# Decoder layer on one core: the context's rounding and that of two batches moved beside the attention

## The chip, the cores and the metric
The kernel runs on one core of one Trainium2 chip. The metric is the time of one execution on the device in microseconds (us), lower is better. Engines are named TensorE (PE in the rows, PEld its weight loads), VectorE (DVE), ScalarE (ACT), GpSimd (POOL) and SyncE (SP, which issues nearly all transfers).

## What is computed
One decoder layer on x, four batches of 512 tokens, width 512, in float32. Cut to what matters:

```python
x = x + attention(layernorm(x), wq, wk, wv, wo)    # 32 heads, 8 key heads, head width 64, rotary, causal
xq = quant_dequant_act_1x128(layernorm(x))         # q = (xb * 448/amax).astype(float8_e4m3fn), back to float32
wq = quant_dequant_weight_128x128(ctx)             # the same, amax over blocks of 128x128 of the context
x = x + einsum('emk,enk->emn', xq, wq)             # each batch with its own context, 512x512
x = x + moe(layernorm(x), ...)                     # 8 experts, top 1, capacity 256, plus a shared feed-forward, width 704
```

The rounding to an 8-bit float is done in float32: the tile is scaled, a step is formed from each element's exponent, the step (a large number) is added and taken away again, and the tile is scaled back.

## The kernel before
All matrix products are made of three products of high and low halves, so most results go through a copy (high half, ScalarE) and a subtraction (low half, VectorE or GpSimd). Each engine has its own program, written out by hand; order within an engine is the order of the code, and engines meet at semaphores. `Once` leaves out a wait whose value was already waited for.

**Attention.** A unit is a group of four query heads of one batch. There are 32 units, so NH = 128 heads, and batches 0 and 1 are complete after unit 15. All engines run the loop `for h in range(-8, NH + 7)`. In iteration h TensorE makes the scores of head h in four blocks (lines 418, 419), a part of the projections of a unit two units ahead (400 to 402), the product with the values of head h-3 (457, 458), the turns of the probabilities of head h-2 (442) and the output of an earlier head. VectorE masks the four score blocks (994), joins halves (1029), makes the low halves of the turned probabilities (1035), adds to X (1044), and once in eight heads splits weights (973). ScalarE takes the exponentials (742) and the high halves (754), and after the probabilities the pair's high half OTh (764). GpSimd normalises the probabilities (1390), rotates queries and keys and makes low halves (1428 for OTl). Projections end with iteration 119.

**The second part.** It follows a table, `slots()`, which gives stages numbers s. Up to s = -9 they run in iteration h = s + 143 of the attention loop (h from NH-11 = 117), three after it, and from s = -5 on beside `ffn(x, k)`, with s = 8x + k - 5; x counts groups of 256 tokens of the shared feed-forward, then experts. For each batch b, 16 slots apart, the stages are:
- `context_max` (1069): the largest magnitudes of the four context tiles, then `context_all` (1454): one `partition_all_reduce` on GpSimd, then `context_scales`. The context is loaded a second time for the rounding.
- `context_round`, per tile: VectorE scales it (1056), isolates the exponent (1062) and forms the step (1064), and GpSimd adds, subtracts and scales back (1433, 1435, 1437); then `context_turn`, four transposes on TensorE (392), a copy on ScalarE (770), a subtraction on VectorE (1106).
- `stats2`, `norm2`: mean and variance of X after attention; `cross_round`, per tile: norm (943), magnitudes (1095), scales (1047 to 1052), and the same rounding; then `cross_turn` and `cross_product`.
- norms, turns and choice of the expert for the routing.

The tiles of the second part live in `work`, whose memory is shared with the attention's tiles. `T1[0]` is also the source of zeros that SyncE writes to `xd`, the experts' input in DRAM, in iterations 116 to 123 (line 1683). `xnx`, two tiles in the attention's memory, is used for the first norms of X only. The first norms and turns of batches 2 and 3 run in iterations 51 to 59.

## Time and profile before

| | us |
|---|---|
| median of 3 runs | 1612.6 (1609.4 to 1612.7) |
| the profiled execution | 1614.8 |
| its span in the profile | 1613.0 |
| TensorE busy | 1467.1 |
| VectorE busy | 1237.6 |
| GpSimd busy | 1058.6 |
| ScalarE busy | 917.9 |

The span is cut in the text by time from its start. Heads of attention run from about 55 to 1020 us, the second part begins beside the last of them at 913 us, and the experts follow at about 1360 us. Busy is time in which an engine executed something; a busy TensorE is not one at its peak, and its granted clock, given for each window as a share of 2.4 GHz, tells how fast it went.

### The profile page before, as it was taken

To read this page: it belongs to the slowest core of one execution; us is meant where nothing else is said; L and a number is where in the kernel's file an instruction comes from. 1 tells how busy PE (TensorE), PEld (TensorE's weight loads), DVE (VectorE), ACT (ScalarE), POOL (GpSimd) and SP (SyncE) were. 2 spreads that over 40 slices of the span, in tenths; PEclk is the share of its full clock that TensorE was granted. 3 is DMA by queue.
4 is the path that set the end of the run, shared out by engine and by line. 5 is a ranking of instruction groups with operands and counts; after the bars stand their busy time and mean duration, and the time that the engine had idled before them with its cause. 6 is when DMAs were issued, how large, how long until landed. Compare 5 with 4: busy or idle time off the path is not lost.

```text
span 1613.0 us, 26858 instructions
## 1 busy us (share of the span) xinstructions
PE 1467.1 (91%) x8616; PEld 1290.2 (80%) x8616; DVE 1237.6 (77%) x2986; ACT 917.9 (57%) x2277; POOL 1058.6 (66%) x1040
## 2 busy tenths in 40 slices
PE   5899999999989999999999967728889898899997
PEld 4688888888878888888888856627778787899996
DVE  6787787788887787788787879858797964677785
ACT  2587777777667777777777655422121213566562
POOL 1798888888776888888888767626252522444545
PEclk9899999999999999999999988969989899899998
DMA  5322232222312222232322333031101003577767
GB/s 189 87 73 66 81 76 71 77 81 55 81 50 63 75 74 66 81 89 55 82 76 59 112 119 92 8 125 41 52 27 53 7 27 113 160 234 221 226 209 239
DMA packets 78796, 152.13 MB, mean 94 GB/s; under 512 B 15366, under 2 KB 15622, under 8 KB 78656
## 3 DMA queue, kind: packets, MB, share of 16 engines
q1 hardware_dynamic: 76096, 142.16, 30.3%
q0 software_dynamic: 2560, 8.25, 1.5%
q8 instruction: 70, 1.15, 0.3%
q14 instruction: 70, 0.57, 0.1%
HBM read 87.58 MB, written 16.78 MB: 65 GB/s over the span
## 4 chain that ended last, share of the span: by engine, by line
PE 74%; DVE 12%; issue 6%; POOL 4%; ACT 2%; DMA 1%; SPq 1%; DVEq 0%; POOLq 0%; ACTq 0%
PE bank L400 15%; PE bank L401 15%; PE bank L402 15%; PE bank L442 7%; PE bank L418 5%; PE bank L457 5%; PE bank L458 5%; PE bank L419 4%; PE bank L392 2%; DVE work L943 1%; POOL P L1390 1%; DVE work L1056 1%; DVE aam L1095 1%; PE bank L429 1%; DVE st L938 1%
## 5 line engine op out<-in xcount | busy, mean ns | idle before, releaser
L742 ACT ACTIVATE P<-P,mn 128x512 f32<-128x512 f32 (+3 forms) x512 | 284.5, 556 | 221.6 <-DVE mn L994 220.9
L1390 POOL TENSOR_TENSOR P<-P,ri 128x128 f32<-128x128 f32 (+3 forms) x512 | 353.9, 724 | 10.4 <-DVE ri L983 10.4
L994 DVE CUSTOM_DVE_ANT_0 P<-bank,mask 128x512 f32<-128x512 f32 (+3 forms) x512 | 235.6, 479 | 118.3 <-PE bank L419 117.9
L1035 DVE TENSOR_TENSOR PTl<-bank,PTh 128x512 fp32r<-128x512 f32 (+1 forms) x384 | 229.2, 598 | 37.0 <-ACT PTh L754 33.9
L442 PE MATMUL bank<-ident,P 128*128 128x128 f32 x1280 | 203.4, 274 | 7.2 <-POOL P L1390 7.2
L754 ACT ACTIVATE PTh<-bank 128x512 fp32r<-128x512 f32 (+1 forms) x384 | 197.6, 516 | 6.0 <-PE bank L442 2.9
L418 PE MATMUL bank<-KT,QT 128*128 128x256 f32 (+2 forms) x512 | 191.2, 373 | 7.4 <-DVE mn L994 7.3
L457 PE MATMUL bank<-PTh,VS 128*128 128x256 f32 (+2 forms) x512 | 164.5, 332 | 11.5 <-DVE PTl L1035 8.8
L400 PE MATMUL bank<-XT,Wh 128*128 128x512 f32 x384 | 165.4, 431 | 9.6 <-DVE qcs L1007 4.7
L419 PE MATMUL bank<-KT,QT 128*128 128x256 f32 (+2 forms) x512 | 167.3, 327 | 0.0
L1428 POOL TENSOR_TENSOR OTl<-Opair,OTh 128x512 fp32r<-128x512 f32 x64 | 83.5, 1305 | 120.8 <-ACT OTh L764 120.5
L458 PE MATMUL bank<-PTl,VS 128*128 128x256 f32 (+2 forms) x512 | 157.4, 329 | 0.0
L442 PEld LDWEIGHTS bank<-ident,P 128*128 128x128 f32 x1280 | 150.9, 141 | 8.0 <-POOL P L1390 7.9
L401 PE MATMUL bank<-XT,Wh 128*128 128x512 f32 x384 | 153.9, 401 | 0.0
L402 PE MATMUL bank<-XT,Wl 128*128 128x512 f32 x384 | 153.8, 401 | 0.0
L1468 POOL TENSOR_TENSOR Ul<-RW,Uh 128x512 fp32r<-128x512 f32 x50 | 73.1, 1465 | 119.4 <-ACT Uh L791 112.0
L457 PEld LDWEIGHTS bank<-PTh,VS 128*128 128x128 f32 x512 | 98.4, 192 | 31.9 <-issue 14.1
L400 PE MATMUL bank<-XT,Uh 128*128 128x256 f32 x352 | 103.7, 295 | 17.2 <-ACT XT L770 10.6
L813 ACT ACTIVATE hm<-bank 128x256 f32<-128x256 f32 x96 | 36.3, 378 | 145.4 <-PE bank L402 133.7
L418 PEld LDWEIGHTS bank<-KT,QT 128*128 128x128 f32 x512 | 98.4, 192 | 24.4 <-DVE mn L994 10.8
L400 PE MATMUL bank<-Oh,OTh 128*128 128x512 f32 x256 | 102.3, 399 | 14.8 <-DVE Opair L1029 9.2
L419 PEld LDWEIGHTS bank<-KT,QT 128*128 128x128 f32 x512 | 99.2, 194 | 10.0
(190 smaller groups left out, 4214.5 us busy)
## 6 DMA issues: line engine op xcount, KB each, us to landing
RW<-in_wf SPq DMA_DIRECT2D x170, 256.0 KB, 3.2
QT<-qh SPq DMA_DIRECT2D x256, 64.0 KB, 2.0
QT<-ql SPq DMA_DIRECT2D x256, 64.0 KB, 2.0
Wraw<-in_wqkv SPq DMA_DIRECT2D x16, 768.0 KB, 4.8
Oraw<-in_wo SPq DMA_DIRECT2D x16, 512.0 KB, 3.4
KT<-KT SPq DMA_DIRECT2D x32, 256.0 KB, 2.9
work<-in_ctx SPq DMA_DIRECT2D x32, 256.0 KB, 2.7
krot<-kvs SPq DMA_DIRECT2D x64, 64.0 KB, 2.0
```

Source lines behind the costliest of these rows:

```text
L400: e.matmul(ps, lh, rh, start=start, stop=False)
L401: e.matmul(ps, lh, rl, start=False, stop=False)
L402: return e.matmul(ps, ll, rh, start=False, stop=stop)
L418: e.matmul(ps[:, 0:k], lhs, KT[:, u % 2, 0, 0:k], start=True, stop=False)
L419: e.matmul(ps[:, 0:k], lhs, KT[:, u % 2, 1, 0:k], start=False, stop=True).then_inc(p_s, 1)
L442: last = e.transpose(ps[:, tokens(m)], src, ident[:, :])
L457: e.matmul(ps[:, q:512], lhs, pt_of(PTh, kb), start=kb == 0, stop=False)
L458: last = e.matmul(ps[:, q:512], lhs, pt_of(PTl, kb), start=False, stop=kb == 3)
L742: e.activation(pq, pq, ACT.Exp, bias=mn[:, z, qb:qb + 1], scale=-1.0, accum_out=rs[:, z, qb:qb + 1]).then_inc(a_exp, 1)
L994: e.tensor_tensor_reduce(P[:, z, off[qb]:off[qb] + k], bank[n % 2][:, 0:k], mask[:, 512 - k:512], -0.125, BIG, ALU.add, ALU.min, mn[:, z, ...
L1035: e.tensor_tensor(pt_part(PTl, part), bank[2 + part][:, 0:128 * n].rearrange("p (m n) -> p m n", n=128), pt_part(PTh, part).bitcast(F32), ...
L1390: e.tensor_tensor(pq, pq, ri[:, z, qb:qb + 1].to_broadcast([128, n]), ALU.mult).then_inc(g_norm, 1)
```

## The change
The maxima of all sixteen context tiles are taken in iterations 3 to 18, one per head, followed by one reduction for all of them in iteration 20 (four before). Then 24 tiles are rounded in the attention, one per three heads: `background()` says that tile j begins in iteration 22 + 3j for the first nine and 34 + 3j for the others, that is 22 to 46 and 61 to 103. Tiles 0 to 15 are the context, 16 to 23 are batches 0 and 1 of X. Of a tile that begins in iteration h, VectorE makes norm, maxima and scales in h (X only); ScalarE scales with four copies in h+1; VectorE forms the steps and GpSimd adds and subtracts in h+2; ScalarE scales back in h+3; SyncE stores it to a new array `kept` in DRAM in h+4. The tile lies in `xnx`, its step in `Zb`, two buffers each. The statistics of batches 0 and 1 move to iterations 72 to 79. In the second part `context_turn` and the `cross_turn` of batches 0 and 1 read tiles loaded from `kept`; batches 2 and 3 keep their `cross_round`. The zeros come from `Zb` and are written in iterations -3 to 4. The diff, cut to its core:

```diff
+NCTX, NBG = 16, 24
@@ slots() @@
-            plan(s - 13 + i if b else s - 3 + i // 2, "stats2", b, i)
+            if b >= 2:
+                plan(s - 13 + i, "stats2", b, i)
+                plan(s - 1 + i, "cross_round", b, i)
             plan(s + 1 + i, "cross_turn", b, i)
-            plan(s - 1 + i, "cross_round", b, i)
...
-            plan(s + i // 2, "context_max", b, i)
-        plan(s + 2, "context_all", b)
-        plan(s + 3, "context_scales", b)
-            plan(at, "context_round", b, i)
-            plan(at + 2, "context_turn", b, i)
+            plan(s + 6 + i + i // 3, "context_turn", b, i)
+def background():
+    return [22 + 3 * j if j < 9 else 34 + 3 * j for j in range(NBG)]
@@ scalar_engine @@
+            def scaled(j):
+                y = xnx[:, j % 2, :]
+                if j < NCTX:
+                    need.wait_ge(v_cscale, 1)
+                    need.wait_ge(d_by[j % 2], 16 * (j // 2 + 9))
+                else:
+                    need.wait_ge(v_bscale, j - NCTX + 1)
+                for c in range(4):
+                    k = wsc[:, 1, 4 * j + c:4 * j + c + 1] if j < NCTX else asc[:, j % 4, 0, c:c + 1]
+                    last = e.activation(y[:, tokens(c)], y[:, tokens(c)], ACT.Copy, scale=k)
+                last.then_inc(a_scaled, 1)
...
                     pair(h - 3)
+                if h - 3 in begins:
+                    unscaled(begins[h - 3])
+                if h - 1 in begins:
+                    scaled(begins[h - 1])
@@ vector_engine @@
                 if t >= 2 * TB:
                     need.wait_ge(p_xt, t - 1)
+                    need.wait_ge(d_keep, 16 * 9)
...
+            def tile_scales(j):
+                t = j - NCTX
+                y = xnx[:, j % 2, :]
+                need.wait_ge(d_keep, 16 * (j - 1))
+                after()
+                chain(normed(y, t))
+                after()
+                chain(e.tensor_reduce(aam[:, j % 4, :], four(y), AX.X, ALU.max, apply_absolute_value=True))
+                after()
+                scales(aam[:, j % 4, :], asc[:, j % 4, 0, :], asc[:, j % 4, 1, :], 1e-4).then_inc(v_bscale, 1)
+
+            def steps_of(j):
+                y, q = xnx[:, j % 2, :], Zb[:, j % 2, :]
+                need.wait_ge(a_scaled, j + 1)
+                if j < 2:
+                    need.wait_ge(d_zero, 16 * NT)
+                else:
+                    need.wait_ge(g_bq, j - 1)
+                chain(e.tensor_scalar(q.bitcast(U32), y.bitcast(U32), 0x7F800000, None, ALU.bitwise_and))
+                after()
+                e.tensor_scalar(q, q, 2.0 ** -6, 1.5 * 2.0 ** 20, ALU.max, ALU.mult).then_inc(v_bq, 1)
...
                     rotate(unit, 1, 1)
+                if 3 <= h < 3 + NCTX:
+                    context_max(h - 3)
+                if h == 21:
+                    context_scales()
+                if 72 <= h < 72 + 2 * TB:
+                    need.wait_ge(v_x, last_x(h - 72) + 1)
+                    stats_of(h - 72)
+                if h == 72 + 2 * TB - 1:
+                    rstd_of(slice(0, 2 * TB))
+                if begins.get(h, 0) >= NCTX:
+                    tile_scales(begins[h])
+                if h - 2 in begins:
+                    steps_of(begins[h - 2])
                 if h >= 0 and h % 8 == 0 and 0 < h // 8 + 1 < NEP:
                     split_wq_lo(h // 8 + 1)
@@ gpsimd_engine @@
+            def background_rounded(j):
+                y, q = xnx[:, j % 2, :], Zb[:, j % 2, :]
+                need.wait_ge(v_bq, j + 1)
+                e.tensor_tensor(y, y, q, ALU.add).then_inc(g_badd, 1)
+                need.wait_ge(g_badd, j + 1)
+                e.tensor_tensor(y, y, q, ALU.subtract).then_inc(g_bq, 1)
...
-                if h == NH - 12:
-                    wait_wraw(need, NEP - 1)
-                    e.memset(T1[0], 0.0).then_inc(g_zero, 1)
+                if h == 20:
+                    need.wait_ge(v_cmax, NCTX)
+                    e.partition_all_reduce(wsc[:, 0, :], wam[:, :, :].rearrange("p i c -> p (i c)"), 128,
+                                           bass.bass_isa.ReduceOp.max).then_inc(g_call, 1)
+                if h - 2 in begins:
+                    background_rounded(begins[h - 2])
@@ sync_engine @@
+            def keep(j):
+                need.wait_ge(a_kept, j + 1)
+                if j >= 1:
+                    need.wait_ge(d_keep, 16 * j)
+                e.dma_start(keptv[j], xnx[:, j % 2, :]).then_inc(d_keep, 16)
...
+                if h in (-4, -3):
+                    load_background(h + 4)
+                if 3 < h < 2 + NCTX:
+                    load_background(h - 2)
+                if h - 4 in begins:
+                    keep(begins[h - 4])
+                if begins.get(h, NCTX) < NCTX:
+                    load_background(NCTX + begins[h])
+                if -3 <= h < 5:
                     for i in range(2):
                         need.wait_ge(g_zero, 1)
-                        e.dma_start(xdz[2 * (h - NH + 12) + i], T1[0]).then_inc(d_zero, 16)
+                        e.dma_start(xdz[2 * (h + 3) + i], Zb[:, 0, :]).then_inc(d_zero, 16)
```

GpSimd in iteration 20, before: keys' rotation, the pair's low half, then the next head's work.

```order
L1408 TENSOR_TENSOR krot<-krot,ksin 64x512
L1411 TENSOR_TENSOR kt<-kt,krot 64x512
L1428 TENSOR_TENSOR OTl<-Opair,OTh 128x512
L1402 TENSOR_TENSOR ql<-qcs,qh 128x1024
L1390 TENSOR_TENSOR P<-P,ri 128x128
```

The same place with the change; `ISA wsc<-wam` is the reduction, the plain `ISA` rows switch GpSimd's code.

```order
L1464 TENSOR_TENSOR krot<-krot,ksin 64x512
L1467 TENSOR_TENSOR kt<-kt,krot 64x512
L1484 TENSOR_TENSOR OTl<-Opair,OTh 128x512
L1576 ISA
L1576 ISA wsc<-wam 128x64
L1458 ISA
L1458 TENSOR_TENSOR ql<-qcs,qh 128x1024
L1446 TENSOR_TENSOR P<-P,ri 128x128
```

The reduction now stands between the pair and the query remainders of the next unit, ahead of the normalisation of head 20.

VectorE in iteration 24, before: join, first low half of the probabilities, weight split, fourth mask.

```order
L1029 TENSOR_TENSOR Opair<-bank,Otmp 64x512
L1035 TENSOR_TENSOR PTl<-bank,PTh 128x512
L973 TENSOR_TENSOR Wl<-Wraw,Wh 128x4x128
L994 ISA P,mn<-bank,mask 128x128
L994 ISA mn 128x1
L1035 TENSOR_TENSOR PTl<-bank,PTh 128x4x128
L1035 TENSOR_TENSOR PTl<-bank,PTh 128x2x128
```

The same place with the change.

```order
L1065 TENSOR_TENSOR Opair<-bank,Otmp 64x512
L1071 TENSOR_TENSOR PTl<-bank,PTh 128x512
L1129 TENSOR_SCALAR Zb<-xnx 128x512
L1131 TENSOR_SCALAR Zb<-Zb 128x512
L1009 TENSOR_TENSOR Wl<-Wraw,Wh 128x4x128
L1030 ISA P,mn<-bank,mask 128x128
L1030 ISA mn 128x1
```

The two steps of the first context tile stand ahead of the weight split, the fourth mask and the two other low halves of the probabilities.

VectorE beside the feed-forward, slots -2 and -1 (batch 1), before: `hm` and `Hl` are the feed-forward's hidden tiles.

```order
L1056 TENSOR_TENSOR work<-work,wsc 128x512
L1062 TENSOR_SCALAR work<-work 128x512
L1064 TENSOR_SCALAR work<-work 128x512
L1106 TENSOR_TENSOR XT<-bank,XT 128x4x128
L1224 TENSOR_TENSOR Hl<-hm,Hh 128x256
L1237 TENSOR_TENSOR hm<-hm,bank 128x256
L943 TENSOR_SCALAR work<-X,mv,rstd 128x512
L1095 TENSOR_REDUCE aam<-work 128x4
L1047 TENSOR_SCALAR asc<-aam 128x4
L1049 RECIPROCAL asc<-asc 128x4
L1051 TENSOR_SCALAR asc<-asc 128x4
L1052 TENSOR_SCALAR asc<-asc 128x4
```

The same place with the change.

```order
L1197 CAST ohb<-lq 128x32
L1202 TENSOR_TENSOR cum<-cum,lq 128x8 x4
L1155 TENSOR_TENSOR XT<-bank,XT 128x4x128
L1267 TENSOR_TENSOR Hl<-hm,Hh 128x256
L1280 TENSOR_TENSOR hm<-hm,bank 128x256
```

The context rounding and the norm, maxima, scales and rounding of a cross tile are gone; the next hidden tile follows at once.

## Rows read from the trace of the kernel before

**Rows 1.** The page: busy us (share of the span) xinstructions of an engine.
```profile
PE 1467.1 (91%) x8616; PEld 1290.2 (80%) x8616; DVE 1237.6 (77%) x2986; ACT 917.9 (57%) x2277; POOL 1058.6 (66%) x1040
```

**Rows 2.** Windows of the span: busy time of each engine, clock, DMA.
```profile
core 0: us, PE busy (x) PEld busy (x) DVE busy (x) ACT busy (x) POOL busy (x), PEclk, DMA share, GB/s
200.00:400.00 200.00, 200.00 (x1159) 175.78 (x1158) 160.10 (x434) 149.94 (x390) 168.34 (x178) 1.00 0.28 73
913.00:1019.00 106.00, 77.85 (x397) 64.74 (x397) 88.92 (x225) 58.33 (x150) 77.11 (x80) 0.87 0.35 106
1019.00:1061.00 42.00, 32.50 (x152) 26.26 (x153) 37.12 (x80) 12.32 (x23) 18.43 (x16) 0.91 0.15 48
1061.00:1088.00 27.00, 3.78 (x17) 3.03 (x16) 11.69 (x31) 7.88 (x16) 8.27 (x11) 0.56 0.34 102
1088.00:1136.00 48.00, 37.03 (x225) 33.77 (x225) 41.86 (x86) 9.57 (x21) 29.45 (x24) 0.89 0.13 41
...
1190.00:1218.00 28.00, 19.88 (x97) 16.70 (x96) 26.81 (x54) 4.22 (x10) 17.84 (x15) 0.82 0.03 9
...
930.00:960.00 30.00, 19.02 (x99) 15.83 (x98) 19.37 (x47) 15.51 (x41) 17.14 (x19) 0.83 0.40 130
```

**Rows 3.** Timeline, VectorE: start, length, operation; heads 113, 117, 128 begin.
```profile
883.90 0.17 DVE L983 RECIPROCAL ri<-rs 128x4 f32<-128x4 f32 x1
...
913.02 0.17 DVE L983 RECIPROCAL ri<-rs 128x4 f32<-128x4 f32 x1
...
1019.19 0.17 DVE L983 RECIPROCAL ri<-rs 128x4 f32<-128x4 f32 x1
```

**Rows 4.** Timeline, GpSimd: last normalisation, first reduction, what follows it.
```profile
930.53 3.20 POOL L1390 TENSOR_TENSOR P<-P,ri 128x128 f32<-128x128 f32 x4
939.28 0.39 POOL L1454 PARTITION_ALL_REDUCE wsc<-wam  x1 [5.55 <-issue]
946.84 1.25 POOL L1395 TENSOR_TENSOR qcs<-qcs,q2s 128x512 f32<-128x512 f32 x1 [7.17 <-issue]
```

**Rows 5.** Lines 1062, 1064 (VectorE) and 1433, 1435 (GpSimd): min/median/max, then means.
```profile
L1062 DVE TENSOR_SCALAR work<-work x32: 426/427/1398, 952.6 to 1296.2; 128x512 uint32<-128x512 uint32 x32
...
L1062 DVE TENSOR_SCALAR work<-work 128x512 uint32<-128x512 uint32 x6 | 5.4, 906 | 0.2
L1064 DVE TENSOR_SCALAR work<-work 128x512 f32<-128x512 f32 x6 | 5.0, 834 | 0.2
...
L1435 POOL TENSOR_TENSOR work<-work 128x512 f32<-128x512 f32 x32 | 43.6, 1361 | 2.5
L1433 POOL TENSOR_TENSOR work<-work 128x512 f32<-128x512 f32 x32 | 41.3, 1290 | 74.1 <-DVE work L1064 74.1
```

**Rows 6.** Groups by form, 200 to 420 us: busy, mean ns, idle before.
```profile
L994 DVE CUSTOM_DVE_ANT_0 P<-bank,mask 128x256 f32<-128x256 f32 x31 | 13.2, 425 | 32.0 <-PE bank L419 32.0
...
L1035 DVE TENSOR_TENSOR PTl<-bank,PTh 128x256 fp32r<-128x256 f32 x30 | 12.7, 425 | 8.2 <-ACT PTh L754 8.2
...
L1428 POOL TENSOR_TENSOR OTl<-Opair,OTh 128x512 fp32r<-128x512 f32 x15 | 19.5, 1299 | 29.8 <-ACT OTh L764 29.8
...
L754 ACT ACTIVATE PTh<-bank 128x256 fp32r<-128x256 f32 x30 | 10.9, 364 | 0.0
```

**Rows 7.** Timeline: a last subtraction and its use; a cross tile from norm to scaling.
```profile
298.21 0.42 DVE L1035 TENSOR_TENSOR PTl<-bank,PTh 128x256 fp32r<-128x256 f32 x1 [0.22 <-ACT PTh L754]
...
300.28 0.39 PE L457 MATMUL bank<-PTh,VS 128*128 128x512 f32 x1
...
999.77 1.14 DVE L943 TENSOR_SCALAR work<-X,mv,rstd 128x512 f32<-128x512 f32 x1
...
1002.35 0.69 DVE L1056 TENSOR_TENSOR work<-work,asc 128x512 f32<-128x512 f32 x1
```

**Rows 8.** DMA issues: what, count, KB each, us to landing.
```profile
xd<-work SPq DMA_DIRECT2D x16, 256.0 KB, 3.6
```

140 lines of the change are left out of this document (73 added, 67 removed).

## The prediction

> **What bounds the kernel now.** I read the page's busy shares first: TensorE 91%, VectorE 77%, GpSimd 66% [rows 1]. These are averages over stages with different limits, so the windows come next [rows 2]. From 200 to 400 us, plain attention, TensorE shows no idle time at clock 1.00, and VectorE is busy 160 us of 200, ScalarE 150, GpSimd 168. Attention is bound by TensorE, with three engines close behind. From 913 us on it is different: TensorE is busy 77.85 of 106 us at 0.87, then 32.5 of 42 at 0.91, 3.78 of 27 at 0.56, 37.03 of 48 at 0.89. That is 223 us with 151 us of matmul time, part of it at the lower clock. In these windows lies the rounding of two batches, which the change removes from them. The starts of heads say the same: four heads from 883.90 to 913.02 us take 7.28 us each, eleven from 913.02 to 1019.19 take 9.65 us each [rows 3], though the last eight have no projections left for TensorE.
>
> So the change trades time in which TensorE starves for extra work in a stage where it doesn't. What counts is how much of the new work fits under its matmuls there.
>
> **The gain, stage by stage.** Busy time multiplied by granted clock estimates what TensorE needs at full clock.
> 1. 913 to 1019: 77.85 x 0.87 = 68 us, against 106 [rows 2]. The change takes from VectorE here the maxima, four context roundings, two of the four cross roundings, statistics and a call of the reduction across partitions on GpSimd, and puts back only four copies and four subtractions for the turns. The zero writes also leave. The other engines don't all keep exactly up with TensorE, so of the 38 us I take 36.
> 2. 1019 to 1061: 32.5 x 0.91 = 30 us, against 42. Two cross roundings go, and the maxima and statistics of batch 1, but the last outputs are added and the statistics after the cross product are computed as before. Of 12 us I take 9.
> 3. 1061 to 1088: TensorE waits for the first pieces of the feed-forward weights, whose low halves GpSimd computes; GpSimd is behind its second reduction. One call holds it for 13.1 us: its last normalisation ends at 930.53 + 3.20 = 933.73, the next instruction starts at 946.84, and the reduction shows as only 0.39 us between [rows 4]. The second call sits in this window and is on the path. Constants and weight loads stay. I take 13.
> 4. 1088 to 1136: 37.03 x 0.89 = 33 us, against 48. All four cross roundings and the context roundings of batch 1 go. I take 13 of 15.
> 5. Batches 2 and 3 keep their cross rounding: 1190 to 1218 has 19.88 us of TensorE in 28 us [rows 2], and a like window stands 82 us later. Only the context rounding ahead of it goes, so the first cross rounding starts earlier. 4 us each, 8 together.
>
> Sum of gains: 36 + 9 + 13 + 13 + 8 = 79 us; the bounds are about 60 (if VectorE and the hand-offs keep half of stages 1, 2 and 5) and 90.
>
> **The cost in attention.**
> *The reduction.* It is now called once, behind the pair of head 17 in iteration 20, with the query remainders and the normalisation of head 20 queued behind it on GpSimd. The same hold gave TensorE 30 - 19.02 = 11 us of idle time in 930 to 960, at clock 0.83 [rows 2]. VectorE's context scales wait for it in iteration 21, ahead of the last mask and two of the probability subtractions; that wait is shorter than GpSimd's and mostly inside the same stall. I take 11 us and 3 for the clock: 14. The ends are 5, if GpSimd's lead hides more, and 20.
> The Trainium skill, GPSIMD Engine Reference, section 2.1, puts the first call of a freshly loaded kernel at about 6 us of code loading. The trace has 933.73 to 939.28 for that part, 5.6 us, but also 7.2 us after the instruction, which the page does not mention; by the page alone the cost would be 7 us smaller.
>
> *The steps of a tile on VectorE.* Each of 24 tiles adds a mask of the exponent and a maximum with a multiplication. Alone such an instruction takes 0.43 us (median), at worst 1.40; from 913 to 1019, with GpSimd busy 73% of the time, the two took 0.91 and 0.83 on average [rows 5]. So VectorE is held while GpSimd works on memory. In attention GpSimd is at 84% and will be higher. I take 2.1 us for the pair, bounds 0.9 and 2.8.
> What hides it: VectorE's idle time in 220 us, 31 heads, is 32.0 us before the third mask and 8.2 us before the last subtraction [rows 6], together 1.3 per head. But most of it lies ahead of the place of the new steps or in the next head. Directly, the last probability subtraction ends at 298.21 + 0.42 = 298.63 and TensorE uses it at 300.28 [rows 7]: 1.65 us of room. A pair of steps of 2.1 overruns that by about half a microsecond. 24 x 0.5 = 12 us.
> *The eight cross tiles* also have norm, maximum and scales, from 999.77 to 1002.35, 2.6 us [rows 7]. With GpSimd always busy I take 3.4, an overrun of 1.8 each: 14 us. In these heads VectorE's idle time of three heads, 3.9 us, is less than the 5.5 us added, so at least 1.6 us a tile must come out, however smooth it is.
> *Pile-ups.* Four pairs of steps fall on a head that also has the weight subtraction of VectorE, and the statistics of eight tiles, one per head, end in a chain of small instructions for the scales. I take 7 us.
> *GpSimd* adds an addition and a subtraction, 1.29 + 1.36 us [rows 5], in three heads of 21.8 us: from 84% to 96%. It waits 29.8 us for OTh in 220 us [rows 6], which takes up most of that. But the joining of the halves on VectorE waits for the same GpSimd instruction. *ScalarE* adds eight copies of 128x128; a copy of 128x256 takes 0.36 us [rows 6], so under 2.9 us in three heads, against a quarter of its time idle. The sixteen context maxima sit one per head and fit the room. For these three together 5 us.
> *SyncE* adds 40 loads and 24 stores, each with a wait for an earlier head. Behind them stand the next query and key placements, which start later than what is waited for. Nothing. The added wait before the norms of the second half is for the store of tile 8, issued an iteration earlier; nothing. The zero writes, 3.6 us each to landing [rows 8], now share the queues with the first query placements, where TensorE is not yet full. 3 us, bounds 0 and 8.
>
> Sum of costs: 14 + 12 + 14 + 7 + 5 + 3 = 55 us, bounds 25 and 85. The net is 79 - 55 = 24 us. The profiled execution took 1614.8 us, its span 1613.0; it stands 2.2 us above the median of the three runs, 1612.6. 1614.8 - 24 = 1591, against the median 1589.
>
> **Rivals.**
> *A: the cover holds.* The steps mostly meet pauses of GpSimd and take 0.9 us, below the 1.65 us of room. For it speaks the median of 0.43; against it GpSimd at 96%. Then only the reduction, some 8 us for the cross tiles and the start remain, 25 us: 1614.8 - 79 + 25 = 1561, so 1559.
> *B: the gain goes to the next wait.* Once the roundings are gone, heads 120 to 127 are still paced by the hand-offs between VectorE and TensorE, and the switch to feed-forward by the weights. For it speaks that VectorE is busy 37.12 of 42 us in the second window [rows 2], of which only about 16 leave. Gain 57, cost 55: 1611.
> *C: slower.* VectorE is the place. The added instructions are 24 x 2.8 for steps at the upper bound, 8 x 3.4 for the cross tiles, 16 x 0.7 for maxima and some 10 for statistics: 116 us. If in-order waiting passes them on to TensorE almost one for one, the cost is 14 + 3 + 0.8 x 116 = 110, against 79: 1644. It decides the sign once more than about 62 of these 116 us (79 less 17) come out. Against it speaks that a weight subtraction (line 973) already stands at the same place on VectorE every eighth head, and TensorE shows no idle time [rows 2].
> The Trainium skill, GPSIMD Engine Reference, section 8, says that the GpSimd shares its memory interfaces with VectorE and that instructions in a two-port mode or with two inputs in SBUF contend; that is the mechanism under C, and the durations above agree with it.
> *D: it doesn't do what it says.* A wait in SyncE's queue for a tile's store delays the query placements in every third head. 24 x 1.5 us more, 1625. Nothing in the order speaks for it.
>
> **How the numbers follow.** Forecast, 1575 to 1605: 0.55. A: 0.15. B: 0.13, half of it still over 0.2% faster. C: 0.12. D: 0.05. A measurement of this kernel can tell about 0.2%, 3 us, from no change. Faster 0.55 + 0.15 + 0.07 = 0.77, same 0.06, slower 0.12 + 0.05 = 0.17. The range leaves out C, D and the far end of A: 1559 to 1616. The predicted time is the forecast's, 1589.
>
> **What would show it.** Right: heads 117 to 128 at 6 to 6.6 us each, one hold of GpSimd of 13 us near 200 us with TensorE idle for about 11, no idle stretch of 25 us before the feed-forward, and heads with a tile in attention 0.5 us longer, from iteration 82 on 2 to 3 us longer every third head, with VectorE's probability subtraction as what TensorE waits for. Wrong: steps at 0.43 us beside a busy GpSimd (then A), or heads longer also between tiles (then C), or eleven heads still above 8 us without roundings (then B).

## The result

The changed kernel takes 1652.3 us (median of 4 runs, 1649.2 to 1653.8), the kernel before 1612.0 beside it (4 runs, 1609.4 to 1612.7). The ratio is 1.025, 95% interval 1.023 to 1.027. The change makes the kernel slower by 2.5%; the forecast was 1589, 1.4% faster.

The profiled execution of after has a span of 1647.4 us. Its page (busy us, share of the span, instructions), against [rows 1]:

```profile
PE 1471.0 (89%) x8616; PEld 1268.5 (77%) x8616; DVE 1224.7 (74%) x2939; ACT 974.2 (59%) x2469; POOL 1027.2 (62%) x1013
```

VectorE and GpSimd are busy for less time than before. Totals don't tell where it went; the starts of iterations do. The reciprocal of the sums (now line 1019) is VectorE's first instruction in an iteration of the loop over heads, as in [rows 3]. Iterations 117 and 128 begin here:

```profile
1023.85 0.17 DVE L1019 RECIPROCAL ri<-rs 128x4 f32<-128x4 f32 x1
...
1101.70 0.17 DVE L1019 RECIPROCAL ri<-rs 128x4 f32<-128x4 f32 x1
```

Iteration 117 begins at 913.02 before and at 1023.85 now: the attention became 110.8 us longer. From there to the end it was 700.0 us and is 623.6: 76.4 us are gained. The sum of the two is the result, 34 us in the traces and 40 between the medians.

Where both lie, from the starts of the iterations (us; "tiles" are the background tiles whose steps fall there):

| iterations | before | after | more | what was added |
|---|---|---|---|---|
| 1 to 20 | 138.4 | 144.7 | 6.3 | context maxima, loads, zero writes |
| 21 to 23 | 21.3 | 34.3 | 13.0 | reduction across partitions |
| 24 to 52 | 213.6 | 237.6 | 24.0 | 9 context tiles |
| 53 to 62 | 86.84 | 86.85 | 0.0 | nothing |
| 63 to 71 | 65.1 | 71.6 | 6.5 | 3 context tiles |
| 72 to 81 | 73.5 | 92.6 | 19.1 | 4 context tiles, statistics of 8 tiles |
| 82 to 107 | 188.6 | 231.4 | 42.7 | 8 cross tiles |
| 117 to 127 | 106.2 | 77.9 | -28.3 | |
| 128 to batch 2's first cross norm | 173.5 | 136.8 | -36.7 | |
| from there to the end | 420.3 | 408.9 | -11.4 | |

The rest is 0.2 us more in iterations 108 to 116 and 1.0 us less before iteration 1. In iterations 24 to 107, 92.3 us longer in all, TensorE's idle time rises from 9 to 70 us. Its granted clock, 1.00 before, is 0.98 there: in six stretches, 27 us together, it is at 1.2 GHz, the first from 257.0 us on, just behind a wait of TensorE of 2.03 us. At most 14 of the 92 us are that clock (an estimate: half of 27).

The windows (busy time and count of each engine, TensorE's clock, DMA share, GB/s), against [rows 2]: the first two are the attention, which had no idle TensorE; the third is iterations 117 to 127, where it now has 68 us of matmul time in 78 at 1.00 of the clock, against 78 in 106 at 0.87.

```profile
200.00:240.00 40.00, 29.77 (x155) 25.71 (x154) 22.78 (x64) 21.73 (x57) 23.00 (x26) 0.87 0.17 41
240.00:400.00 160.00, 149.68 (x823) 126.78 (x822) 125.52 (x322) 120.50 (x325) 136.10 (x138) 0.98 0.34 92
1024.00:1102.00 78.00, 67.94 (x400) 57.06 (x398) 60.09 (x168) 57.52 (x150) 52.79 (x61) 1.00 0.31 87
```

What TensorE waits for in the attention of after (total us, times, longest), 230 to 470 us and then 726 to 951 us:

```profile
PE bank L464 <- DVE X L1080: 12.2, 13, 2.0
PE bank L425 <- DVE mn L1030: 2.1, 4, 1.1
...
PE bank L464 <- DVE X L1080: 15.2, 18, 1.2
PE bank L425 <- DVE mn L1030: 13.0, 11, 2.9
```

The first is not the instruction that the forecast named. Line 464 (457 before) writes the weighted values into bank 5. The output projection goes through the same bank, and VectorE's last instruction of an iteration, the addition into X (line 1080, 1044 before), must have read it. In the kernel before, the row between the two of [rows 7] is this one:

```profile
299.15 0.68 DVE L1044 TENSOR_TENSOR X<-X,bank 128x512 f32<-128x512 f32 x1
```

It ends at 299.83, and TensorE uses the bank at 300.28: the room was 0.45 us, not 1.65. It is no exception: from 200 to 425 us, in the kernel before, this room is between 0.15 and 0.62 us in every iteration.

GpSimd's reduction, its predecessor and its successor, against [rows 4]:

```profile
202.84 1.29 POOL L1484 TENSOR_TENSOR OTl<-Opair,OTh 128x512 fp32r<-128x512 f32 x1 [1.19 <-ACT OTh L795]
209.85 0.54 POOL L1576 PARTITION_ALL_REDUCE wsc<-wam  x1 [5.72 <-issue]
217.93 2.33 POOL L1458 TENSOR_TENSOR ql<-qcs,qh 128x1024 fp32r<-128x1024 f32 x1 [7.54 <-issue]
```

From 204.13 to 217.93 GpSimd does nothing else: 13.8 us, 13.1 before.

VectorE's added instructions, against [rows 5] (line, count, min/median/max ns, first and last start):

```profile
L1129 DVE TENSOR_SCALAR Zb<-xnx x24: 408/538/1495, 242.2 to 940.1; 128x512 uint32<-128x512 uint32 x24
L1131 DVE TENSOR_SCALAR Zb<-Zb x24: 426/1260/1402, 243.1 to 940.7; 128x512 f32<-128x512 f32 x24
L1117 DVE TENSOR_REDUCE aam<-xnx x8: 686/686/687, 731.6 to 922.5; 128x4 f32<-128x512 f32 x8
L1083 DVE TENSOR_SCALAR asc<-aam x16: 170/394/1526, 732.3 to 1336.6; 128x4 f32<-128x4 f32 x16
L1085 DVE RECIPROCAL asc<-asc x16: 177/178/180, 732.8 to 1336.8; 128x4 f32<-128x4 f32 x16
```

The steps (1129, 1131) reach 1.4 to 1.5 us, and a multiplication of 128x4 elements also takes up to 1.53. The maximum over 128x512 and the reciprocal of 128x4 never vary. So the length of some instructions depends on something other than their size.

### The profile page after: what moved, and what is told of

Same layout as the page of the kernel before. It is cut to its first block, busy times and chain, and to the rows that moved or that the text cites. A ratio compares the mean times of both kernels' runs of the same rounds, so it can differ in the third digit from the quotient of the medians.

```text
span 1647.4 us, 27010 instructions
## 1 busy us (share of the span) xinstructions
PE 1471.0 (89%) x8616; PEld 1268.5 (77%) x8616; DVE 1224.7 (74%) x2939; ACT 974.2 (59%) x2469; POOL 1027.2 (62%) x1013
## 4 chain that ended last, share of the span: by engine, by line
PE 52%; DVE 21%; ACT 13%; issue 8%; POOL 3%; DMA 1%; SPq 1%; DVEq 0%; POOLq 0%; ACTq 0%
PE bank L407 11%; PE bank L408 11%; PE bank L409 11%; PE bank L449 5%; ACT P L752 4%; PE bank L464 4%; PE bank L465 4%; DVE PTl L1071 3%; PE bank L425 2%; PE bank L426 2%; ACT PTh L764 2%; DVE X L1080 2%; DVE P L1030 2%; PE bank L399 2%; DVE Zb L1131 1%
## 5 line engine op out<-in xcount | busy, mean ns | idle before, releaser
L1446 POOL TENSOR_TENSOR P<-P,ri 128x128 f32<-128x128 f32 (+3 forms) x512 | 358.5, 732 | 29.1 <-DVE ri L1019 27.3
L464 PE MATMUL bank<-PTh,VS 128*128 128x256 f32 (+2 forms) x512 | 169.9, 342 | 55.5 <-DVE X L1080 47.0
L425 PEld LDWEIGHTS bank<-KT,QT 128*128 128x128 f32 x512 | 97.6, 191 | 55.8 <-DVE mn L1030 41.0
L465 PEld LDWEIGHTS bank<-PTl,VS 128*128 128x128 f32 x512 | 99.9, 195 | 7.8
```

Source lines behind the costliest of these rows:

```text
L425: e.matmul(ps[:, 0:k], lhs, KT[:, u % 2, 0, 0:k], start=True, stop=False)
L464: e.matmul(ps[:, q:512], lhs, pt_of(PTh, kb), start=kb == 0, stop=False)
L465: last = e.matmul(ps[:, q:512], lhs, pt_of(PTl, kb), start=False, stop=kb == 3)
L1446: e.tensor_tensor(pq, pq, ri[:, z, qb:qb + 1].to_broadcast([128, n]), ALU.mult).then_inc(g_norm, 1)
```

## The experiments

Times are medians; the medians of the kernel before beside them were 1611.5 to 1614.8, and each ratio is to the one taken beside it. "Attention" is the start of iteration 117, against 913.0 before and 1023.9 after.

### Taking parts of the added work away

**Steps on one column** (VectorE's two instructions; `q[:, 0:1]` in place of `q`, `y` alike):

```
- e.tensor_scalar(q, q, 2.0 ** -6, 1.5 * 2.0 ** 20, ALU.max, ALU.mult)
+ e.tensor_scalar(q[:, 0:1], q[:, 0:1], 2.0 ** -6, 1.5 * 2.0 ** 20, ALU.max, ALU.mult)
```

> Leaves out work: VectorE's two step instructions (mask of the exponent, maximum with multiplication) touch one column of 512 in each of the 24 background tiles, so the roundings are wrong; waits, copies, GpSimd's addition and subtraction, loads and stores stay. The changed kernel takes 1652; its attention is 110.9 us longer up to iteration 117. Theory T1 (the room on VectorE): TensorE's next product waits for the addition into X that stands last on VectorE in an iteration, which had only 0.45 us of room, and the steps push it back by more. Then most of what the 24 tiles cost apart from norm, maximum and scales goes: 2.0 us for each of 16 context tiles and 2.0 for each of 8 cross tiles, about 45 us, 1607. Theory T2 (GpSimd): the addition and subtraction on GpSimd (2.65 us a tile) delay its query and key halves and hold VectorE; the steps are only where it shows: 12 us or less gained, 1640. T3 (copies on ScalarE, transfers, waits of the queues): no gain over 5 us, 1648.

Measured: 1621.4, ratio to before 1.005 (1.003 to 1.008). 31 us gained, between T1 and T2; attention 29.9 us shorter.

**GpSimd's addition and subtraction on one column:**

```
- e.tensor_tensor(y, y, q, ALU.add)
+ e.tensor_tensor(y[:, 0:1], y[:, 0:1], q[:, 0:1], ALU.add)
```

> Leaves out work: GpSimd's addition and subtraction touch one column of 512 in each of the 24 background tiles, so the roundings are wrong; all else stays. T1 (VectorE's own added instructions overrun its room): they shrink only by what GpSimd's traffic adds to them, 20 us gained, 1632. T2 (GpSimd is the cause, by its delay of the query halves and by its traffic): 42 us or more, 1610 or below. T3: no gain over 5 us.

Measured: 1635.7, ratio 1.014 (1.011 to 1.017). 17 us gained, near T1. Neither engine's part is all of it. The iterations show that they act at different places: iteration 27, which holds steps, is 8.79 us in after, 8.72 without GpSimd's part and 7.19 without the steps (6.94 before); iteration 25, which holds none, is 9.41, 7.54 and 9.42 (7.53 before). Iteration 26 loses its extra time, 8.41 against 6.91, when either part is gone. Iteration 25 is the second of a group of four, with a tile's addition and subtraction queued at the end of 24. Behind them stands the query remainder, on which VectorE's next rotation and then the addition into X wait, and TensorE for that:

```profile
252.76 2.38 POOL L1458 TENSOR_TENSOR ql<-qcs,qh 128x1024 fp32r<-128x1024 f32 x1
...
255.27 0.69 DVE L1043 TENSOR_TENSOR qcs<-bank,rope 128x512 f32<-128x512 f32 x1 [1.78 <-POOL ql L1458]
255.88 0.68 DVE L1080 TENSOR_TENSOR X<-X,bank 128x512 f32<-128x512 f32 x1
...
256.70 0.50 PE L464 MATMUL bank<-PTh,VS 128*128 128x512 f32 x1 [2.03 <-DVE X L1080]
```

**All the arithmetic of the background tiles on one column** (steps, GpSimd, ScalarE's eight copies, cross norm and maximum):

> Leaves out work: in all 24 background tiles the steps, GpSimd's addition and subtraction, ScalarE's eight copies and the norm and maximum of the cross tiles touch one column (one per block), so the roundings are wrong. Loads, stores, every wait, the sixteen context maxima, the statistics and the reduction across partitions stay. If the arithmetic on the three engines is the cost (T1 and T2 alike), what is left of 110.9 us in attention is start 5, reduction 13, statistics and fixed costs of small instructions some 15: 1652 - 78 = 1574, between 1562 and 1590. If transfers and waits of SyncE matter (T3), it stays above 1610.

Measured: 1595.4, ratio 0.989 (0.986 to 0.992), 57 us gained where 78 were expected. What stays in the attention is 51 us: start 7, reduction 13.5, iterations 24 to 71 6, 72 to 81 10.3, and still 16.1 in 82 to 107, though the cross tiles have only their small instructions left there. One of them, on VectorE:

```profile
862.86 0.27 DVE L1115 TENSOR_SCALAR xnx<-X,mv,rstd 128x1 f32<-128x1 f32 x1
863.16 0.16 DVE L1117 TENSOR_REDUCE aam<-xnx 128x4 f32<-128x4 f32 x1
863.35 0.69 DVE L1083 TENSOR_SCALAR asc<-aam 128x4 f32<-128x4 f32 x1
864.08 0.18 DVE L1085 RECIPROCAL asc<-asc 128x4 f32<-128x4 f32 x1
864.29 0.99 DVE L1087 TENSOR_SCALAR asc<-asc 128x4 f32<-128x4 f32 x1
865.20 1.30 DVE L1088 TENSOR_SCALAR asc<-asc 128x4 f32<-128x4 f32 x1
...
866.76 0.44 PE L425 MATMUL bank<-KT,QT 128*128 128x384 f32 x1 [2.00 <-DVE mn L1030]
```

Three multiplications and maxima of four elements per partition take 3.0 us together. The size of the work isn't what they cost.

**No reduction across partitions:**

```
- e.partition_all_reduce(wsc[:, 0, :], wam..., 128, bass.bass_isa.ReduceOp.max)
+ e.tensor_tensor(wsc[:, 0, :], wam..., wam..., ALU.add)
```

> Leaves out work: the one reduction of the context maxima across partitions is replaced by a small addition on GpSimd, so the scales of the context are wrong; all else stays. The iterations around it were 12.7 us longer than before the change (the forecast had 14). If the hold of GpSimd by the reduction is all of it: 1652 - 12.7 = 1639, and GpSimd shows no gap of 13 us near 205 us. If VectorE's wait for it or the two buffers of the maxima matter too, some of the 12.7 stays: 1645.

Measured: 1637.3, ratio 1.015 (1.010 to 1.020). 15 us gained; iterations 21 to 23 fall from 34.3 to 22.8 us, attention by 12.3. The term of the forecast was right.

### Moving work

**Steps and cross scales ahead of the second block's mask** (order of VectorE's queue in an iteration; the whole computation, as in the next three):

```
+ if begins.get(h, 0) >= NCTX: tile_scales(begins[h])
+ if h - 2 in begins: steps_of(begins[h - 2])
  masked(h, 1)
  ...
- if begins.get(h, 0) >= NCTX: tile_scales(begins[h])
- if h - 2 in begins: steps_of(begins[h - 2])
  masked(h, 0)
```

> The whole computation, other order: VectorE's steps and the cross tiles' norm, maximum and scales stand ahead of the mask of the second query block (before it VectorE waits 0.9 us per head for TensorE's scores, 70 us in the 79 heads from 230 to 951), not behind the query rotation ahead of the last mask. Theory (room by place: what matters is whether the added time lies before or behind VectorE's wait in an iteration): 0.9 of the 1.7 us of a pair of steps is hidden, so 15 us of the 30 that the steps cost, and 5 more in the cross tiles: 1632. Rival (no place has room: the later second mask delays the exponentials on ScalarE and with them TensorE's scores): no gain or slower, 1650 to 1660.

Measured: 1628.4, ratio 1.010 (1.007 to 1.012). 24 us gained without a single operation less. The place counts, but not as the theory had it. It put 15 us on the steps and 5 on the cross tiles; the iterations give 2.6 us in 24 to 71, where only context tiles are, 3.5 in 72 to 81, and 17.4 in 82 to 107, where norm, maximum and scales moved with the steps. Among the context tiles the iterations with steps got shorter (27 from 8.79 to 7.17 us), and others longer (33 from 9.30 to 10.54): there the steps are held, now ahead of the join, and TensorE waits for the join in place of the addition into X.

```profile
313.90 2.47 DVE L1131 TENSOR_SCALAR Zb<-Zb 128x512 f32<-128x512 f32 x1
316.64 0.68 DVE L1065 TENSOR_TENSOR Opair<-bank,Otmp 64x512 f32<-64x512 f32 x1
...
317.46 0.47 PE L407 MATMUL bank<-Oh,OTh 128*128 128x512 f32 x1 [2.61 <-DVE Opair L1065]
```

**Context alone in the background** (NBG = 16; statistics, norm and rounding of batches 0 and 1 planned behind the heads as before):

> The whole computation: the sixteen context tiles are rounded beside the attention as in the changed kernel, but the eight cross tiles of batches 0 and 1 (statistics, norm, maximum, scales, rounding) stay behind the heads as before the change. What this tells is what the cross tiles cost (42.7 us in iterations 82 to 107, some 12 more in 72 to 81 for the statistics) and bring. Theory (the cross tiles are the part that doesn't pay): attention 55 us shorter, of the 76 us gained behind the heads about 33 come back: 1652 - 55 + 33 = 1630. Rival (most of the gain behind the heads comes from the cross rounding): 55 or more come back, 1652 or above. Other rival (the context and the reduction carried it): 15 come back, 1612.

Measured: 1625.8, ratio 1.007 (1.003 to 1.010). Attention is 52.3 us shorter, and from iteration 117 to the end 655.0 us against 623.6: 31.4 come back. The cross tiles of the two batches, their statistics included, cost 52 and bring 31.

**Steps in two iterations:**

> The whole computation: as the run with the earlier place, and the two step instructions of a tile stand in two iterations, one each ahead of the second block's mask; GpSimd's addition and subtraction, the copies back and the store follow one iteration later. Theory (room by place): each of the two (0.68 and 1.06 us mean) fits the 0.9 us, so nearly all of the 30 us that the steps cost goes, and about 5 in the cross tiles: 1620. If the earlier place has no room: as the other run, 1650 to 1660.

Measured: 1650.2, ratio 1.022 (1.019 to 1.026). The expectation was wrong by 30 us. Iterations 24 to 27 fell to 8.1, 7.5, 6.9 and 8.9 us, but iteration 33 took 14.5. VectorE's and GpSimd's rows there:

```profile
309.61 6.19 DVE L1129 TENSOR_SCALAR Zb<-xnx 128x512 uint32<-128x512 uint32 x1
315.72 0.41 DVE L1030 CUSTOM_DVE_ANT_0 P<-bank,mask 128x256 f32<-128x256 f32 x1
...
309.21 1.27 POOL L1437 TENSOR_TENSOR Wl<-Wraw,Wh 128x512 fp32r<-128x512 f32 x1
310.45 2.36 POOL L1463 TENSOR_TENSOR ql<-qcs,qh 128x1024 fp32r<-128x1024 f32 x1
312.77 2.74 POOL L1451 TENSOR_TENSOR P<-P,ri 128x128 f32<-128x128 f32 x4
```

An instruction that takes 0.41 us at its shortest starts 0.4 us after one of GpSimd's and ends 0.3 us after a gapless run of six of them, 6.19 us later. TensorE waits 5.3 us there.

**The maximum across partitions on VectorE** (in outline):

```
+ e.transpose(Zb[:, 1, 0:64], wam)            # 32x32 blocks
+ e.tensor_reduce(wgm, wtr, AX.X, ALU.max)    # per group of 32 partitions
+ store 1 KB, load to all partitions, tensor_reduce over the 4 groups
- partition_all_reduce
```

> The whole computation: the maximum across partitions is made by VectorE (a transpose of 32x32 blocks and a maximum within each group of partitions), a store of 1 KB, a load of it to all partitions and a maximum over the four groups, in place of GpSimd's reduction. Theory (the cost near iteration 21 is GpSimd's hold by the reduction alone): 12.7 to 15 us gained, 1638. Rival (VectorE's added small instructions and SyncE's wait for the store take half of it back): 1645.

Measured: 1642.0, ratio 1.017 (1.012 to 1.023). 10 us gained, iterations 21 to 23 at 22.9 us. Between the two expectations: the hold goes from those iterations (11.4 us less), and attention as a whole is 9.6 us shorter.

**One tile per four heads.** Context only, the maximum on VectorE, and each part at a fixed place in the group of four iterations: steps in the first, ahead of the second block's mask, GpSimd in the second, copies back in the third, store in the fourth. Beside it the same with the steps back at the late place:

```
- return [22 + 3 * j if j < 9 else 34 + 3 * j for j in range(NBG)]
+ return [22 + 4 * j if j < 6 else 62 + 4 * (j - 6) for j in range(NBG)]
...
- if h - 2 in begins: background_rounded(begins[h - 2])
+ if h - 3 in begins: background_rounded(begins[h - 3])
```

> The whole computation. Context only beside the attention, one tile per four heads so that every part has a fixed place in its group of four iterations: VectorE's steps and the context maxima ahead of the second block's mask, the steps in the first iteration of a group, GpSimd's addition and subtraction in the second (not in the first, where the query halves stand behind them), the maximum across partitions by VectorE and a small store and load; cross tiles behind the heads as before the change. Theory (place and phase): what stays in attention is the start 6, the maximum 2, the steps 0.6 for each of 16 tiles (the run with the earlier place showed 0.6, 0.0 and 0.6 us in iterations 24, 36 and 48), GpSimd and copies 3, so 21 us; the gain behind the heads without the cross tiles is 76.5 - 31.5 = 45: 1613 - 24 = 1589, faster than the kernel before. If holding of VectorE by GpSimd is as strong in any phase: steps 2.7 for each of 16, 43 + 11: 1622.

> The whole computation, as the run beside it, with the two step instructions back at the place of the changed kernel (behind the query rotation, ahead of the last mask), still in the first iteration of a group. What it tells apart: place against phase. Theory (room by place): about 1.1 us more for each of 16 tiles, 18 us above the other. If the phase alone did it, the two are within 4 us of each other.

Measured: early place 1594.6 against 1611.5, ratio 0.989 (0.987 to 0.991), **faster than both kernels**; late place 1627.2, ratio 1.010 (1.007 to 1.012). Several things changed at once between this kernel and those above; what the pair shows is the place. The fixed phase by itself brought nothing: with the late place iterations 24 to 107 take 682.7 us, against 668.6 in the kernel with context alone and one tile per three heads; with the early place they take 647.6. The difference of the pair is 33 us where 18 were expected, and 21.5 of it stand in eight iterations that hold no steps: 31, 39 and 47, then every eighth from 71 to 103 (h mod 8 = 7), take 10.4 to 11.0 us against 7.9 to 8.1. There VectorE has the subtraction of the output weights (line 1016, both inputs in SBUF), in the late kernel:

```profile
344.95 4.27 DVE L1016 TENSOR_TENSOR Ol<-Oraw,Oh 128x512 fp32r<-128x512 f32 x1 [0.95 <-ACT Oh L720]
349.15 0.41 DVE L1031 CUSTOM_DVE_ANT_0 P<-bank,mask 128x256 f32<-128x256 f32 x1
...
343.42 1.29 POOL L1489 TENSOR_TENSOR OTl<-Opair,OTh 128x512 fp32r<-128x512 f32 x1
344.68 1.28 POOL L1443 TENSOR_TENSOR Ol<-Oraw,Oh 128x512 fp32r<-128x512 f32 x1
345.93 2.74 POOL L1451 TENSOR_TENSOR P<-P,ri 128x128 f32<-128x128 f32 x4
```

4.25 to 4.30 us in eight of them, ahead of a mask; 0.69 in the kernel before, 1.35 with the early place.

### What holds VectorE

**That subtraction on one column:** `Ol[:, 1, 0:1]` in place of `Ol[:, 1, :]`, inputs alike.

> Leaves out work: in the kernel with one tile per four heads and the steps at the late place (1627), VectorE's subtraction for the low half of the output weights touches one column of 512 in all but the first of its sixteen calls, so the later results are wrong. In the trace of that kernel this instruction, whose two inputs both lie in SBUF, took 4.25 to 4.30 us in eight calls during the tiles (0.69 us in the kernel before, 1.35 in the run with the early place), until GpSimd's run of four normalisations ended. Theory (the holding of one existing instruction by GpSimd's run is most of what the late place costs): the eight iterations with h mod 8 = 7 fall from 10.6 to about 7.5 us: 25 us gained, 1602. If the long duration only fills time that VectorE would wait through anyway: 5 us or less, 1623.

Measured: 1623.6, ratio 1.007 (1.005 to 1.009), 3.6 us gained, the rival's number. But the row says that the edit did not do what it should:

```profile
344.55 3.74 DVE L1017 TENSOR_TENSOR Ol<-Oraw,Oh 128x1 fp32r<-128x1 f32 x1 [0.95 <-ACT Oh L720]
...
345.52 2.75 POOL L1452 TENSOR_TENSOR P<-P,ri 128x128 f32<-128x128 f32 x4
```

One element per partition, and still 3.74 us, to 348.29; GpSimd's run ends at 348.27. So the question stayed open, and this was asked next.

**A one-source instruction of one element in its place:**

```
- e.tensor_tensor(Ol[:, 1, :], Oraw[:, 1, :], Oh[:, 1, :].bitcast(F32), ALU.subtract)
+ e.tensor_scalar(rtmp[:, 0:1], rtmp[:, 0:1], 1.0, None, ALU.mult)
```

> Leaves out work: in the kernel with one tile per four heads and the steps at the late place (1627), fifteen of VectorE's sixteen subtractions for the output weights are replaced by a one-source instruction of one element per partition; all waits stay. The earlier run with a two-input instruction of one column left its duration at 3.74 us, so it did not take the holding away. One-source instructions of one element took 0.15 us wherever they stood. Theory (the holding of this instruction by GpSimd's run is most of what the late place costs): the iterations with h mod 8 = 7 fall from 10.6 to about 7.5 us, 25 us gained, 1602. Rival (TensorE and the exponentials wait there for something else): at most 6 us gained, 1621 or more.

Measured: 1601.7, ratio 0.992 (0.990 to 0.995). 25 us gained, as the theory had it. The instruction takes 0.144 to 0.155 us all 15 times, and iterations 31, 39 and 47 fall to 7.9 to 8.0 us. One held instruction in eight iterations was most of what the late place cost. In iterations 24 to 107, 28 us shorter, TensorE's idle time falls by 17 us (39.6 to 22.3), and its clock, 0.98 with the held instruction, is 1.00 without: part of the price of a wait is the clock behind it. What is left of the late place is 7 us for 16 tiles (654.6 against 647.6 us with the early one), less than half of the 18 that room by place had given.

**Steps on two columns** in the changed kernel, beside the run with one:

> Leaves out work: the changed kernel with the two step instructions on two columns of 512 in each of the 24 tiles, beside the run with one column (1621.4 against 1652.3 for the full ones). One column is never held (0.15 us in all 24), two or more can be. Theory (holding by GpSimd, not the size of the work, is the larger part of the steps' cost): durations scatter between 0.15 and 1.3 us, mean 0.5 or more, and about half of the 31 us comes back: 1637. Rival (the size of the work is the cost): durations near 0.15 us, 1622 to 1626.

Measured: 1637.7, ratio 1.014 (1.010 to 1.019). The rows of the run with one column (busy us, mean ns):

```profile
L1131 DVE TENSOR_SCALAR Zb<-Zb 128x1 f32<-128x1 f32 x23 | 3.5, 154 | 0.8
L1129 DVE TENSOR_SCALAR Zb<-xnx 128x1 uint32<-128x1 uint32 x23 | 3.3, 142 | 0.0
```

and with two:

```profile
L1129 DVE TENSOR_SCALAR Zb<-xnx 128x2 uint32<-128x2 uint32 x24 | 13.2, 551 | 0.0
L1131 DVE TENSOR_SCALAR Zb<-Zb 128x2 f32<-128x2 f32 x24 | 11.7, 487 | 0.8
```

A second column costs 0.74 us a pair and 16 us of the kernel (17 in attention; the two runs lie 12 us apart, 1631.7 and 1643.8). Two elements take 0.16 and 0.17 us at their shortest, so it isn't their size: about half of the 31 us that the steps cost comes from holding alone. Whether the other half is the size of a full instruction or more holding isn't told apart.

### Two attempts at more

**ScalarE's copies in mid iteration:**

> The whole computation, as the kernel with one tile per four heads and the early place (1594.6), with ScalarE's eight copies of a tile moved from the end of an iteration to ahead of the exponential of the second block, where ScalarE waits for VectorE's mask. In that kernel the iterations with h mod 8 = 7 are 1.0 us longer than before the change and those with h mod 8 = 0 1.4 us, and the weight copy of ScalarE stands there directly behind the tile's copies. Theory (the copies delay the weight halves): 10 to 15 us gained, 1582. Rival (the copies of 1.3 us are longer than the wait of 0.9 there and delay the exponential): no gain or up to 6 us slower, 1595 to 1601.

Measured: 1605.9, ratio 0.996 (0.994 to 0.998); 11 us slower than the kernel it starts from, more than even the rival said. Iteration 26 goes from 6.91 to 7.81 us and 39 from 7.99 to 9.25. That ScalarE's time ahead of a mask isn't free because the exponential behind it is needed at once is a reading; the run shows only that the copies cost more there.

**Context maxima one iteration later:**

> The whole computation: the kernel with one tile per four heads and the early place (1594.6), with the context maxima and their loads one iteration later. In its trace VectorE waited 3.8 us once for such a load, in iteration 7 (9.94 us against 6.73 before the change). Theory (that wait is most of what the start still costs): 3 to 5 us gained, 1590. Rival (the transfers of the zero writes crowd the query placements, whatever VectorE does): within 1.5 us, 1594.

Measured: 1594.5, ratio 0.988 (0.986 to 0.989): the same time as 1594.6. But the edit didn't take away the wait that it was made for. VectorE waits for a load in iteration 7 here too, 3.40 us against 3.80, and TensorE behind it 2.22 us against 2.71; the iteration is still 9.4 us:

```profile
101.12 0.69 DVE L1105 TENSOR_REDUCE wam<-xnx 128x4 f32<-128x512 f32 x1 [3.40 <-DMA xnx<-in_ctx]
...
102.89 0.47 PE L410 MATMUL bank<-Oh,OTh 128*128 128x512 f32 x1 [2.22 <-DVE Opair L1066]
```

So the run decides nothing about that wait. Nor is it a gain that iterations 1 to 20 fell by 2.7 us, from 145.4 to 142.7: the kernel with the late place has the same code there as the one with the early place and takes 142.6.

## Why the prediction was wrong

**The gain was right**: 79 forecast, 76.4 measured. By stage: iterations 117 to 127 28.3 against 36, the stages up to batch 2 36.7 against 35, batches 2 and 3 11.4 against 8. Part of the closeness is luck, since the first stage fell short by 8 and the others gave 5 more than forecast. The iterations take 7.1 us each, not 6 to 6.6; from 1024 to 1102 us TensorE still waits for VectorE and ScalarE, most for the probability subtraction (once 2.8 us). That is rival B's mechanism, for 8 of its 22 us.

**The costs were forecast at 55 and measured 110.8.** The reduction and the start, 17 of the 55, were near. The error lies in iterations 24 to 107: steps, cross tiles, pile-ups and most of the 5 for GpSimd, ScalarE and maxima make 38 us at most, and these iterations became 92.3 us longer.

**The reduction was right**: 14 forecast, 13.0 in the iterations, 12.3 to 15 when taken away.

**The start** was forecast at 3, plus part of 5 for maxima, and measured 6.3. Of this 6.2 lie in iterations 3 to 18, which hold the maxima. The maximum (0.69 us) stood behind the query rotation like the steps, and didn't fit the room: iterations 9 to 18 took 72.6 us before, 75.2 here, and 72.9 to 73.4 in all kernels with the maxima ahead of the second block's mask. The other 3.6 us, in iterations 3 to 8, stay with either place.

**The steps were mis-sized, and here the prediction fell.** The step that failed is the room on VectorE. The prediction took 2.1 us for a pair against 1.65 us of room, an overrun of half a microsecond, 12 us for 24. The pair took 1.72 us (0.71 and 1.01 on average), less than forecast. But the room was 0.45, because the probability subtraction in [rows 7] isn't VectorE's last instruction that TensorE waits for. With that room the overrun is 1.27 us and the term 30 us (an estimate from the two numbers); taking the steps away gave 31, and of the nine iterations that hold them from 24 to 48, seven got 1.2 to 1.75 us shorter and two 0.6. Those rows were in the trace: the next one on VectorE and what else writes bank 5 had to be read. The agreement is closer than the argument: with two columns, too short to overrun unless held, half of the 31 us was still there, so the average pair hides how uneven the holding is. With all its parts, on GpSimd and ScalarE too, a context tile cost 2.5 us (30.5 us for the 12 tiles of iterations 24 to 71).

**The cross tiles** had the same room and the same mistake: 2.3 us a tile with the steps, 18 us in all. Iterations 82 to 107 became 42.7 us longer, 5.3 a tile with GpSimd's and ScalarE's part. The sentence that 5.5 us added can't fit 3.9 us of idle time was right in kind. The scales were mis-sized too: norm, maximum and scales, "2.6 us, with GpSimd always busy 3.4", were 4.6 us in the tile at 865.54, with 1.48 for one instruction of 128x4.

**Pile-ups** were forecast at 7. The statistics alone took some 6 us in iteration 79, where a chain of 128x8 instructions of 0.17 us each had four of 0.6 to 1.2.

**The clock** had a term of 3 us with the reduction and none for the waits of TensorE further on, where it was 0.98.

**GpSimd** was priced as time that fits into its idle time. It does (from 230 to 470 us it waits 26.2 us for OTh, 29.7 before), but two other things count: the query remainder behind a tile's work in the first iteration of a group (1.0 to 1.9 us, once per four tiles), and, as a reading of the held rows, that every gap it loses is one in which VectorE could have run a held instruction. Taken away, GpSimd's part gave 17 us, where it shared 5 with ScalarE's copies and the maxima.

**SyncE** was priced at nothing, and rival D got no support in size: loads, stores and their waits stay in the run without arithmetic, and TensorE's waits there from 230 to 900 us are for VectorE. Only once does TensorE wait for a transfer, 2.2 us for keys at 53.8 us, before iteration 1; all changed kernels have this wait (1.5 to 3.3 us), the kernel before hasn't. Iteration 1 of the changed kernel begins 1.0 us earlier all the same.

**Rival C came true**, with 0.12. Its time was 1644 and its price of 110 us in attention is the 110.8 measured, though the exact agreement is luck. It had 93 us for all that VectorE gets (steps, cross scales, maxima, statistics), as 0.8 of 116; VectorE's busy time in iterations 24 to 107 rose by only 78 us, these iterations by 92, and C had no price for GpSimd's part, whose removal gave 17. Its mechanism, that in-order waiting passes the added work on almost one for one, is what the rows show at the late place, and so is its sign, longer iterations between those with steps (25 and 26, 1.9 and 1.5 us). What spoke against it in the prediction, that a weight subtraction stands there every eighth head without TensorE being idle, was no evidence: the windows of [rows 2] showed TensorE just busy, not how near it was to waiting.

The Trainium skill, SBUF — State Buffer, section "SBUF: two separate sides", says of the pair of interfaces that VectorE and GpSimd share that it is an exclusive lock for the whole instruction, taken by a VectorE instruction in a two-port mode or with two inputs in SBUF (the latter only against a GpSimd instruction that reads SBUF). The traces agree in the forms: one source with two or more elements, or two SBUF inputs, are held; a reduce, a reciprocal, one source with one element (0.13 to 0.16 us) or an operand in PSUM are not. They differ in the length: VectorE waited not for one GpSimd instruction but for gapless runs of up to six (6.19 us).

What stays open: which of the two engines wins when both are ready, and so which VectorE instruction falls on GpSimd's long run. For one instruction that decided 25 us, and it was found by trying. Nor is it settled what 3.6 of the start's 6.3 us are, nor how much of the cross tiles' 42.7 us is holding.

## What to carry to other kernels

Before work is put into a full engine's queue, read the room at the last instruction in that queue for which the bound engine waits, and compare places: the same instructions cost 24 us less ahead of a wait of VectorE than behind it, though mostly for the long cross tiles. Then look at what the new work makes longer elsewhere: a VectorE instruction that GpSimd can hold costs up to GpSimd's gapless run beside it, not its own size, and the one that is held may be an old one. Gaps in GpSimd's queue beside it should help; that was not tried by itself.

The kernel that turned the loss of 2.5% into a gain of 1.1% has context tiles only, the early place, the maximum on VectorE and a tile period (four, not three) that matches the loop. The period made the cost of each place readable, and so the held instruction could be found; it was no gain by itself, since with the late place this kernel is 1.0% slower than the kernel before.

## What the runs showed of the hardware

- One-source VectorE instructions on SBUF: one element per partition 0.13 to 0.16 us every time (0.26 to 0.27 for the norm with its two operands per partition); two elements 0.16 to 1.7 us; four elements up to 1.53 in the changed kernel; 128x512 0.41 us at its shortest and up to 6.19.
- With two SBUF inputs even one element per partition was held for 3.74 us. In all seventeen traces the maximum over 128x512 took 0.65 to 0.69 us, the reciprocal of 128x4 0.16 to 0.18, and the 128x512 instructions that read a bank 0.65 to 0.69.
- The hold of GpSimd by a reduction across partitions lasts past the instruction: 5.7 us ahead of it, 7.5 behind. A transpose and two maxima on VectorE with a transfer of 1 KB gave 10 us of it back.
- Many iterations repeat to 0.03 us between different kernels where nothing of them was changed (iteration 53: 9.21 to 9.24 us in all seventeen), so single iterations of two profiles can be compared, far below what the whole time can tell. Some don't: iteration 56 lies between 10.20 and 10.77 us in the changed kernels, and the kernels with the late and the early place, alike up to iteration 23, differ by 2.8 us in iterations 1 to 20, where the clock is 1.00 and 0.98. So a difference is read from several iterations, with the clock beside it.
